# Gate weights in one resident load, LoRA-A weights converted once and loaded from SyncE's queue (transformer block, 8 cores)

## The reference

```python
h  = layernorm(x)
q  = h @ Wq.T                                  # 32 heads of 128
lat = [h @ Wk_down.T, h @ Wv_down.T]           # 8 groups of 32 + 32
k, v = k_cmp @ Wk_up.T, v_cmp @ Wv_up.T        # 8 kv heads, each used by 4 heads
x1 = x + layernorm(causal_softmax(q k / sqrt(128)) v @ Wo.T)
xf = layernorm(x1)
base   = xf @ base_W.T                         # 4096 x 4096
logits = xf @ gate_W.T                         # 28 experts
gate_full = softmax over the top 2 logits, 0 elsewhere
hA  = einsum('nd,erd->ner', xf, lora_A)        # 28 experts x rank 8 = 224 columns
hA  = hA * (gate_full * 2)[:, :, None]
out = x1 + layernorm(base + einsum('ner,eor->no', hA, lora_B))
```

## Time and profile before

| what | value |
|---|---|
| device time, median of 3 runs | 5537.42 us |
| the three runs | 5545.31, 5327.59, 5537.42 us |
| the profiled execution | 5336.24 us |
| its slowest core's span (core 1) | 5335.1 us |
| spans of the 8 cores | 5222.7 to 5335.1 us |
| TensorE busy | 3058.4 us, 57% of the span |
| VectorE, ScalarE, POOL busy | 1527.3, 1030.0, 210.2 us |
| DMA queue of POOL / of SP, share of 16 engines | 31.4% / 22.6% |

### The profile page before, as it was taken

One profiled execution on the slowest core, in us unless ns is written; L12 is line 12 of the kernel. 1 busy time (PEld: TensorE's weight loads), 2 busy tenths in 40 slices (PEclk: granted clock), 3 DMA queues, 4 the chain that ended last, 5 costly groups with the idle time before them and its releaser, 6 DMA issues.

```text
span 5335.1 us, 37122 instructions; the slowest of 8 cores (5222.7 to 5335.1 us)
## 1 busy us (share of the span) xinstructions
PE 3058.4 (57%) x13056; PEld 1199.2 (22%) x13056; DVE 1527.3 (29%) x2250; ACT 1030.0 (19%) x977; POOL 210.2 (4%) x324
## 2 busy tenths in 40 slices
PE   0211202202202978898943890888998989991594
PEld 0100100001101432233421340332332333340242
DVE  1101011111011005665031014015666666204103
ACT  0100000000001004453011002004554555002001
POOL 1000001001000000000002000000000000000100
PEclk9855656656656999999975995999998999995697
DMA  9999999999999551001623557451000000351364
GB/s 120 126 118 125 125 126 114 121 127 120 126 122 113 150 142 33 1 1 36 170 79 47 152 152 116 144 143 39 1 1 1 1 1 17 104 164 34 78 168 136
DMA packets 640403, 492.15 MB, mean 92 GB/s; under 512 B 418000, under 2 KB 626896, under 8 KB 626912
## 3 DMA queue, kind: packets, MB, share of 16 engines
q0 software_dynamic: 163744, 199.74, 31.4%
q1 hardware_dynamic: 476480, 290.03, 22.6%
HBM read 604.93 MB, written 119.54 MB: 136 GB/s over the span
## 4 chain that ended last, share of the span: by engine, by line
PE 51%; SPq 19%; DMA 14%; DVE 6%; ACT 5%; issue 3%; DVEq 1%; POOLq 0%; POOL 0%; ACTq 0%
SPq L211 19%; PE psz L426 7%; PE pss L461 6%; PE psa L336 4%; PE psa L723 4%; PE psb L723 4%; PE psa L545 4%; PE psb L545 4%; DMA UFMA<-UTM 4%; PE psb L336 4%; PE psb L433 3%; PE psa L433 3%; DVE BSTAT L187 3%; DMA WPb<-WKVD 2%; PE psb L276 2%
## 5 line engine op out<-in xcount | busy, mean ns | idle before, releaser
L276 PE MATMUL psa<-UFMA,WPa 128*128 128x512 bf16 x512 | 146.3, 457 | 1376.2 <-DMA UFMA<-UTM 1328.8
L469 ACT ACTIVATE PTD<-pss 128x1024 bf16<-128x1024 f32 x768 | 741.0, 1021 | 659.8 <-PE pss L461 659.4
L475 DVE TENSOR_TENSOR PTD<-PTD,M 128x2048 bf16<-128x2048 bf16 x384 | 470.3, 1225 | 420.2 <-ACT PTD L469 420.2
L461 PE MATMUL pss<-QFM,KFM 128*128 128x512 bf16 x1536 | 403.9, 380 | 68.4 <-ACT PTD L469 45.4
L187 DVE BATCH_NORM_STATS2 BSTAT<-XA 128x6 f32<-128x512 bf16 x320 | 193.7, 678 | 791.6 <-DMA XA<-X 707.3
L426 PE MATMUL psz<-PTD,E 128*16 128x512 bf16 x1536 | 396.0, 380 | 0.2 <-DVE ACC L448 0.2
L276 PEld LDWEIGHTS psa<-UFMA,WPa 128*128 128x128 bf16 x512 | 57.0, 113 | 1465.0 <-issue 1427.2
L336 PE MATMUL psa<-UFMA,WPa 128*128 128x512 bf16 x1024 | 231.2, 385 | 242.6 <-DMA WPa<-WQB 240.8
L199 ACT ACTIVATE STAT<-STAT 128x1 f32<-128x1 f32 x64 | 13.0, 203 | 1770.0 <-DVEq L197 907.7
L723 PE MATMUL psa<-QFM,WPa 128*128 128x512 bf16 x1024 | 229.8, 383 | 27.9 <-DMA WPa<-BWBMB 27.9
L545 PE MATMUL psa<-QFM,WPa 128*128 128x512 bf16 x1024 | 230.1, 383 | 4.9 <-DMA WPa<-WOB 2.3
(11 more groups left out here) (116 smaller groups left out, 2628.0 us busy)
## 6 DMA issues: line engine op xcount, KB each, us to landing
BWBMB<-BWBM POOLq DMA_DIRECT2D x32, 1088.0 KB, 76.0
XA<-X POOLq DMA_DIRECT2D x32, 1024.0 KB, 57.1
WQB<-WQ POOLq DMA_DIRECT2D x32, 1024.0 KB, 66.0
WOB<-WO POOLq DMA_DIRECT2D x32, 1024.0 KB, 67.4
WPa<-WKVD POOLq DMA_DIRECT2D x16, 1024.0 KB, 53.6
WPb<-WKVD POOLq DMA_DIRECT2D x16, 1024.0 KB, 61.8
OUT<-OSTG SPq DMA_DIRECT2D x16, 1024.0 KB, 4.1
XA<-XOWN POOLq DMA_DIRECT2D x8, 1024.0 KB, 20.2
```

What stands on the lines that cost most here:

```text
L276: ins = TEN.matmul(PSab[pp][:], WP[wp][:, c * 128:(c + 1) * 128], UFMA[:, c * 512:(c + 1) * 512], start=(c == 0), stop=(c == 31))
L461: ins = TEN.matmul(PSS[:, kt * 512:(kt + 1) * 512], KFM[:, kv4 * 512 + kt * 128: kv4 * 512 + (kt + 1) * 128], QFM[:, h * 512:(h + 1) * 512 ...
L469: ins = SCA.activation(PTD[:, ptp * 2048 + hf2 * 1024: ptp * 2048 + (hf2 + 1) * 1024], PSS[:, hf2 * 1024:(hf2 + 1) * 1024], AF.Exp, scale= ...
L475: pm = vS.inc(VEC.tensor_tensor(PTD[:, ptp * 2048:(ptp + 1) * 2048], PTD[:, ptp * 2048:(ptp + 1) * 2048], M01[:], AL.mult))
```

## The change

The gate's weights are loaded in one DMA (GWPF) into the place of M01 and IND16, issued by POOL after the second head group of each chunk, ahead of the Wo stage; the gate loop has no loads left. The LoRA-A weights ATP get 32 conversion jobs of their own into a bf16 tensor ATPB in DRAM, behind the 96 others in the list; the LoRA-A loop's loads read ATPB and are issued by SP in place of POOL, with the same two buffers.

```diff
--- before.py
+++ after.py
@@ -75,6 +75,7 @@
     WQB = nc.dram_tensor("WQB", [32, 32, 128, 128], BF16, kind="Internal").ap()
     WOB = nc.dram_tensor("WOB", [32, 32, 128, 128], BF16, kind="Internal").ap()
     BWBMB = nc.dram_tensor("BWBMB", [32, 34, 128, 128], BF16, kind="Internal").ap()
+    ATPB = nc.dram_tensor("ATPB", [32, 128, 256], BF16, kind="Internal").ap()
     DBGT = None
     if dbg:
         DBGT = nc.dram_tensor("DBG", [512, DM], F32, kind="ExternalOutput").ap()
@@ -119,6 +120,7 @@
     RZB = A("RZB", [16, 512], BF16, O_HSC)
     GST = A("GST", [128, 32], F32, O_GST)
     GWP = A("GWP", [128, 2 * 32], BF16, O_GWP)
+    GWPF = A("GWPF", [128, 32 * 28], BF16, O_M01)
     BSTAT = A("BSTAT", [128, 96], F32, 228480)
     E16 = A("E16", [128, 256], BF16, O_E16)

@@ -150,6 +152,7 @@
     sCVQ = Sem(nc, "sCVQ")
     sCVO = Sem(nc, "sCVO")
     sCVB = Sem(nc, "sCVB")
+    sCVA = Sem(nc, "sCVA")

     def W(eng, *sv):
         for s, v in sv:
@@ -213,7 +216,7 @@
     all_dma_sems = [sXA[0], sXA[1], sWPs[0], sWPs[1], sWPh[0], sWPh[1],
                     sTU[0], sTU[1], sTH[0], sTH[1],
                     sTP, sTHR, sWKV, sGW[0], sGW[1], sAP[0], sAP[1], sST, sRES,
-                    sSTp[0], sSTp[1], sCVQ, sCVO, sCVB]
+                    sSTp[0], sSTp[1], sCVQ, sCVO, sCVB, sCVA]

     def final_waits():
         for s in all_dma_sems:
@@ -227,6 +230,8 @@
         conv_jobs.append((sCVO, WOB[i], WO4[i]))
     for i in range(32):
         conv_jobs.append((sCVB, BWBMB[i], BWBM4[i]))
+    for i in range(32):
+        conv_jobs.append((sCVA, ATPB[i], ATP[i]))
     cv_i = [0]

     def pump_conv(n):
@@ -502,6 +507,10 @@
         ufma_free_v = vS.v
         attn_ready = vS.v
         pss_free_s = sS.v
+        W(GPS, (vS, attn_ready), (tS, tS.v))
+        gwf_ld = sGW[0].inc(GPS.dma_start(
+            out=GWPF[:].rearrange("p (c e) -> p c e", c=32, e=28),
+            in_=GWT.rearrange("c p e -> p c e")), 16)
         if dbg_stage == "attnT":
             stm = 0
             for cc in range(4):
@@ -602,19 +611,12 @@
                          (vS, max(y2r[par], add_marks[tt]))] + ostg_all)
             tr_u(QFM, 512, tt * 128, ybuf[:], [(sS, ap_mark), (tS, qfm_free_t)], par)
         tp_u1 = [(sTU[0], sTU[0].v), (sTU[1], sTU[1].v)]
-        gw_free = [0, 0]
         for c in range(32):
-            gp = c % 2
-            W(GPS, (tS, gw_free[gp]))
-            gm = sGW[gp].inc(GPS.dma_start(out=GWP[:, gp * 32: gp * 32 + 28],
-                                           in_=GWT[c]), 16)
-            W(TEN, (sGW[gp], gm))
             if c == 0:
-                W(TEN, (vS, psab_free[0]), *tp_u1)
-            ins = TEN.matmul(PSab[0][0:28, :], GWP[:, gp * 32: gp * 32 + 28],
+                W(TEN, (sGW[0], gwf_ld), (vS, psab_free[0]), *tp_u1)
+            ins = TEN.matmul(PSab[0][0:28, :], GWPF[:, c * 28:(c + 1) * 28],
                              QFM[:, c * 512:(c + 1) * 512], start=(c == 0), stop=(c == 31))
-            gw_free[gp] = tS.inc(ins)
-        gate_mm = tS.v
+        gate_mm = tS.inc(ins)
         W(VEC, (tS, gate_mm))
         VEC.memset(LOGPAD[:], -30000.0)
         VEC.drain()
@@ -663,9 +665,9 @@
         ap_free = [wp_free[0], wp_free[0]]
         for c in range(32):
             ap2 = c % 2
-            W(GPS, (tS, ap_free[ap2]))
-            am = sAP[ap2].inc(GPS.dma_start(out=WP[0][:, ap2 * 256:(ap2 + 1) * 256],
-                                            in_=ATP[c]), 16)
+            W(SYN, (tS, ap_free[ap2]), (sCVA, sCVA.v))
+            am = sAP[ap2].inc(SYN.dma_start(out=WP[0][:, ap2 * 256:(ap2 + 1) * 256],
+                                            in_=ATPB[c]), 16)
             W(TEN, (sAP[ap2], am))
             if c == 0:
                 W(TEN, (sS, pss_free_s))
```

## The result

The changed kernel takes 0.9868 of the time of the one before, with a 95% interval of 0.9841 to 0.9894: 1.3% less, or some 70 us of 5336. The median of all its 25 executions is 5272.47 us, and the forecast was 5268 us; the same median of the kernel before, over 26 executions, is 5462.78 us. Executions in which the cores of a die ran at a lower granted clock took some 6% longer and are left out of every ratio here but not of the medians (such as the 5537.42 us of before), and of the experiments e2 and e5, whose profiled execution was of this kind, only stretches bound by loads are compared.

What follows compares the result with a forecast made beforehand. The prediction took load round trips, not TensorE or data rate, to bound the gate and LoRA-A loops. Terms -80.2 + 9.2 - 17 + 17 + 3 = -68 us from 5336.24 gave 5268 us, range 5236 to 5490 us.

Steps and rivals of the forecast that it cites:

- gate loop: Gate matmuls without their loads: 32 in a row take 9.4 us per chunk, 80.2 us less over both.
- gap: TensorE between gate and LoRA-A loops: first ATPB load waits behind the logits' transpose, 5.0 us for 0.4, costing 9.2 us.
- LoRA-A loop: LoRA-A matmuls with loads from SP: a round of 3.35 us instead of 3.90, 17 us less over both chunks.
- conversions: 32 new ATPB jobs in the first chunk's own tiles: 2.1 MB on a saturated stretch at 123 GB/s, adding 17 us.
- GWPF: The single gate-weight load beside the first Wo products: delays the third Wo load by 1.5 us twice, 3 us.
- (2): Rival on the first chunk's own tiles: the conversions cost 50 us, giving 5301 us; chance 0.14.
- (4): Rival, slower than before: POOL's backlog starves the own tiles' transposes, outweighing the rest from 85 us on; chance 0.05.
- half pace: Own tiles' transposes: engines alternate between queues, so the backlog could only halve their pace, cost near 17 us or below.
- the forecast's own range: Whole kernel: 5240 to 5300 us, with a landing of 2.0 us give or take 0.3 and conversions of 5 to 35 us.
- Rival (3): Gain over 2%: load lands in 1.5 us, conversions cost 5 us, GWPF nothing, giving 5236 us; chance 0.08.
- (1): Rival on the LoRA-A loop: SP's load lands in 2.9 us, loop costs 12 us more, giving 5299 us; chance 0.10.

Runs made afterwards that it cites:

- e2: The change with the gate loop and its 32 POOL loads put back as before, so the LoRA-A part alone; ratio 0.9985 to the kernel before.
- e5: The change with the ATPB loads issued by POOL in place of SP, still without a cast; LoRA-A loops 59.2 and 59.3 us.
- e1: The change without ATPB: one GWPF load for the gate, LoRA-A weights loaded by POOL with a cast as before; ratio 0.9836 to the kernel before.
- e4: The change with the first two ATPB loads on SP ahead of the logits' transpose; ratio 0.9826 to the kernel before.
- e3: The change with the 32 ATPB conversions issued later, behind the residual's loads at the start of the first chunk's attention; ratio 0.9786 to the kernel before.
- e6: The change with the 32 ATP conversions done twice, the second time into a tensor that nothing reads; own tiles of the first chunk 98.2 us.
- e9: As e7, but the big LoRA-A load waits until the last transposes of the Wo results have landed; ratio 0.9661 to the kernel before.
- e7: The change with all LoRA-A weights in one POOL cast load behind the Wo stage, no ATPB, no loop loads; ratio 0.9699 to the kernel before.

## Why the prediction was right, and where not

The mechanism and the sum of its terms came out: -68 us against 5336.24 us (1.3%), measured 1.3%. The forecast as it stands beside the time shown for before failed.

**The base of the sum, the step that failed.** The -68 us were set against the profiled execution, 5336.24 us, while the time that stands for the kernel before is 5537.42 us. The 201 us between them got no term: the prediction says that it can't place a median in this spread, and states 5268 us all the same. Read against 5537.42 us that is a gain of 4.9%, nearly four times the measured 1.3%. In its place the runs show a spread that the change leaves alone: the 26 executions of before lie between 5300.65 and 5777.68 us (477 us), the 25 of after between 5229.92 and 5701.05 us (471 us), and of the three that were shown, one lies at 5327.59 us and two above 5537. What the sum can forecast is the ratio: 0.9868 of 5336.24 us is 5266 us. That the median of after, 5272.47 us, lies 4 us from the forecast is luck: the same median of before is 5462.78 us, not 5336.

By its steps, for both chunks together:

| step | forecast | measured | shown by |
|---|---|---|---|
| gate loop | -80.2 | -81.1 | table, e1 |
| gap | +9.2 | +8.8 (5.4 against 1.0) | table, e4 |
| LoRA-A loop | -17 | -26.5 | table, e2, e5 |
| conversions | +17 | +14.0 | table, e3, e6 |
| GWPF | +3 | 0 | Wo stage, +0.2 |
| POOL's drain in the attention | no term | +2.6 - 5.1 | rows under the table of stages |

**Gate loop.** The row of 32 matmuls after a long idle time was the right price, clock rise included.

**LoRA-A loop, mis-sized.** The round was put at 3.35 us, from a landing of 2.0 and a reissue of 0.18 us. The trace of after has 1.8 and 0.12 us: 0.26 us less, 4 us over 16 rounds. The 2.5 us that I added for what core 1's loop has above sixteen rounds are not there at the median: 16 rounds of 3.09 us make 49.4, and 49.0 and 48.5 were measured. Before, too, the median loop (61.5 us) is shorter than core 1's (64.4). The 2.15 us that I had worked out from the Trainium skill's "DMA: Bandwidth & Descriptors" (anatomy of one DMA) were further off for SP; the page gives this fit for loads that GpSimd issues, and with those it agrees (2.2 us in e5). Of the signs that I named, the loop of 53 to 58 us and the landing of 2.0 us did not come (49 and 1.8). e5 shows what I could only bound: most of the gain is the queue's, not the cast's.

**Conversions.** 123 GB/s gave 17 us, e6 gives 13 to 14 us for each 2.1 MB. From the fourth own tile's load to the first WQB load it is 59.1 us at the median core, where before had 44.9; the forecast was 63. Rivals (2) and (4) named a price of 50 us and more, and e6 excludes both: with twice the backlog it is 27 us in all. The interaction they rest on is real, though. Landings of the 4 transposes of these tiles, min, median and max, before (core 1) and after (core 3):

```profile
DMA to landing us min/median/max: 5.6/20.4/37.8
```

```profile
DMA to landing us min/median/max: 5.6/30.6/57.5
```

These are different cores. The slowest transpose of a core takes 37.0 us before, 52.6 in after and 63.9 in e6, at the median of the cores; the last two of the four, behind the backlog, take 5.6 us each. So the transposes are held up by the backlog, about as long as it takes to move. That is not the half pace that I derived from the turns between queues in the Trainium skill ("DMA: Bandwidth & Descriptors", queues, rings and completion order). But the loads and conversions must be moved anyway in a stretch that is saturated, and with twice the conversions (e6) the price is twice as high, not more.

**GWPF, mis-sized.** I took the nearest row with as many short rows, 10.5 us at its shortest; it lands in 6.1 us, before the third Wo load is issued. Its rows are four and a half times shorter (56 bytes against 256), and the row of reference was read in a stretch where DMA had other work; no run separates the two.

**The range and the chances.** The range reached up to 5490 us because of the spread of the timed runs; the forecast's own range, 5240 to 5300 us, was the one that the mechanisms supported, and it holds for a kernel of 5336 us before. By calling 2% the limit of what can be told, the text set 0.88 on no difference, while its own terms left hardly a way to come out at zero: the interval of 0.9841 to 0.9894 is clear of 1. Rival (3), a gain over 2%, was not reached, and (1), a landing of 2.9 us, is refuted by the 1.8 us.

**What I had not seen.** The gate's part alone gives the gain to within a few us, and the LoRA-A part nothing that can be told (e1, e2). The numbers for that stood in the sum (-17 + 9 + 17 = +9), and I never added them up by part. The drain on POOL I had not seen at all: the 32 conversions make it 2.6 us longer, and each 32 small loads that leave POOL's queue make the next one 2.6 us shorter.

## What to carry to other kernels

Add a forecast up by part of the diff as well as in total: a part whose terms cancel can be left out, moved to where its transfers are free (e3), or replaced. Where a loop waits for a small load in each step, ask first whether all steps' data fit into a buffer that is free anyway: one load each for gate and LoRA-A, ahead of their loops (e9), made 3.4% together, while the quicker queue for the same small loads, with what it needed, made nothing that can be told (e2). A load moved to another queue inherits whatever waits ahead of it there.

## What was not expected of the hardware

- A plain load of 64 KB issued by SP lands in 1.8 us, issued by POOL in 2.2 us, and with a cast in 2.3 us; after its wait is over, SP issues in about 0.12 us and POOL in 0.49 us (after, e5, before).
- A POOL load of 2 MB beside the last transposes of the Wo results delayed the chain behind them by 2 to 3 us (e7 against e9; it takes 16.3 us itself); transposes beside a saturated POOL queue landed up to 57.5 us after issue (core 3 of after), behind it in 5.6 us.
- 4,096 rows of 28 elements, cast from f32, land in 6.1 us with nothing else on its way (after).
- The granted clock stayed at 1.00 through the LoRA-A loop where it had no loads to wait for and followed the gate loop at once (e7, e9). With a wait for a load in each round it fell to 0.50, with a gap ahead of the loop (after) and without one (e1, e4).
- Between kernels that differ in nothing else ahead of it, a drain on POOL took 2.6 us longer for each 32 DMAs more that POOL had issued: 1.4, 4.0 and 6.6 us behind the end of IND16 in before, after and e6, the same within 0.01 us on all 8 cores.
